# A second round trip through memory for the 256 inverse roots of a gated cross-attention kernel

## The chip, the cores and the metric

One core of one Trainium2 chip runs the kernel. The metric is the device time of one execution in microseconds (us); the time before is 291.95 us, the median of three runs (291.82 to 292.34). On a NeuronCore, TensorE (PE) multiplies matrices, VectorE (DVE) and ScalarE (ACT) work element by element, GpSimd (POOL) does a few small operations here, and SyncE (SP) issues every DMA of this kernel. Each engine runs its own list of instructions in order; engines wait for each other by semaphores.

## The reference

Everything is float32. `x` is 8 x 100 x 1024 (800 rows of width D = 1024), the context 8 x 722 x 512.

```
memory_proj = einsum('bme,de->bmd', memory, W_mem)
scores = einsum('bnd,bmd->bnm', x, memory_proj) / sqrt(D)
mc     = einsum('bnm,bmd->bnd', softmax(scores), memory_proj)
gate   = sigmoid(concat([x, mc]) @ W_gate.T + b_gate)
fused  = x + gate * mc
out    = fused * rsqrt(mean(fused**2, axis=-1) + 1e-6) * norm_w
```

Only the last two lines matter for the change: each of the 800 rows is divided by the root of its own mean square over 1024 columns.

## The kernel before

The kernel never forms `memory_proj`: it multiplies `x` with `W_mem` first, attends in the narrow width 512, and multiplies back. A float32 product is made of three matmuls of split operands (a high part and the rest, `act_hi`/`act_lo`, `w_turn_hi`/`w_turn_lo` and so on). The matrix work is ordered by hand, one list for each engine, with a semaphore for each hand-over.

The end of the program is the gate. The 800 rows fall into three sets:

- rows 0 to 415 (`FIRST`), the **first part**. Model columns lie on the 128 partitions in eight tiles, rows along the free axis;
- rows 416 to 671, the **second part**, 256 rows, in the same layout;
- rows 672 to 799, the **last rows**, 128 of them. Here rows lie on the partitions, and the model columns are worked in three groups of 384, 384 and 256 (`GROUPS`, steps NT, NT + 1 and LAST = NT + 2).

`STEPS` lists the sixteen gate steps of the first two sets, and three more follow for the last rows (`gate_rows`). At each step TensorE makes gate values in PSUM, ScalarE takes the sigmoid (`sigmoid`, lines 777 and 783), VectorE multiplies by `mc` and adds `x` (`gate_times` and `fuse`, lines 1019 and 1024; for the last rows `rows_times` and `rows_fuse`, lines 1046 and 1051), ScalarE squares (lines 814 and 807) and weighs with `norm_w`. For the last rows VectorE does the weighing (`rows_weigh`, line 1057).

For the two parts, the sum of squares runs over partitions, so a row's root has to be brought onto all 128 partitions before VectorE can multiply by it:

- First part: TensorE sums over partitions, VectorE adds the epsilon (line 1083), GpSimd raises to the power -0.5 (line 1151, `rooted`), SyncE stores the roots to a small buffer in device memory `rms_rows` (line 377), waits for that, and loads them back repeated on every partition into `rms_all` (line 379, signal `rms_in`). VectorE then multiplies the eight tiles (`output`, line 1030).
- Second part: two matmuls give the means (`means_second`, line 609), VectorE adds the epsilon (line 1102, `rms_late`), GpSimd takes the power (line 1153, `late_rooted`), and TensorE spreads the roots with two transposes of a broadcast column into a PSUM bank (`turn_roots`, line 616, `rms_turned`), after the first two of the eight blocks of three matmuls of step NT + 1. VectorE multiplies the eight tiles out of that bank (`output_second`, line 1035), five of them after the first group of the last rows, three after the second group.

After the last group VectorE adds up the mean of the last rows (`early_mean`, line 1118, and `rms_last`, line 1125), GpSimd takes the power (line 1155), and ScalarE and VectorE multiply a half each (lines 838 and 1134); two stores (line 390) end the program. The output of the second part leaves in four stores of two tiles each (line 385), each as soon as two products are done (`out_done`).

Of the kernel before, what the change touches and what calls it, by code (L numbers as in the profile page):

```python
# [7 lines left out]
P = 128  # L8
R = B * N
H = R // 2  # L10
KD, KC = D // P, C // P
# [12 lines left out]
FIRST, ROWS = 416, R - P  # L24

SLICES = ((FIRST, FIRST + P), (FIRST + P, ROWS))
# [16 lines left out]
NT = len(STEPS)  # L43
# [7 lines left out]
def build(nc, xT, x_last, ctxT, ctxN, w_mem, w_gate_x, w_mem_t, w_gate_mc, b_gate, norm_w, norm_row, outT, out_rows):  # L51
    F32, F32R = mybir.dt.float32, mybir.dt.float32r
    ALU, ACT, AX = mybir.AluOpType, mybir.ActivationFunctionType, mybir.AxisListType

    top = ExitStack()
    with top:  # L56
        def sb(scope, name, shape, dt=F32):
            return scope.enter_context(nc.sbuf_tensor(name, shape, dt))

        def sem(name):  # L60
            return top.enter_context(nc.semaphore(name))
# [12 lines left out]
        ident = sb(top, "ident", [P, P])  # L74
# [32 lines left out]
        rms_late = sb(top, "rms_late", [P, len(SLICES)])  # L107
# [3 lines left out]
        rms_all = sb(top, "rms_all", [P, TURNED])  # L111
        spread = sb(top, "spread", [P, P])
        same_lane = sb(top, "same_lane", [P, Q])
        square_part = sb(top, "square_part", [P, TURNED // Q])
        rms_rows = nc.dram_tensor("rms_rows", (FC, 4), F32, kind="Internal").ap()


# [22 lines left out]
        def bank(i, cols, rows=P, at=0):  # L140
            return ps[0:rows, i * BANK + at:i * BANK + at + cols]
# [7 lines left out]
        MEANS, RMS = 6, 7  # L149
# [8 lines left out]
        def group_cols(n):  # L158
            t0, t1 = GROUPS[n - NT]
            return slice(t0 * P, t1 * P)  # L160

        def in_tiles(cols):
            return cols.rearrange("p (t c) -> p t c", c=P)

        def gate_bank(n):
            if n >= NT:
                t0, t1 = GROUPS[n - NT]
                return bank(G2B + n % 2, (t1 - t0) * P)
            r0, r1 = STEPS[n][1:]
            return bank(G2B + n % 2, r1 - r0)  # L170
# [49 lines left out]
        squared, weighted = sem("squared"), sem("weighted")  # L220
# [6 lines left out]
        rooted, late_rooted = sem("rooted"), sem("late_rooted")  # L227
        rms_stored, rms_in = sem("rms_stored"), sem("rms_in")
        mean_w_set = sem("mean_w_set")
        late_mean_made = sem("late_mean_made")  # L230
        last_rooted, rms_turned = sem("last_rooted"), sem("rms_turned")
        out_done = sem("out_done")
# [12 lines left out]
        def _(sp):  # L245
# [134 lines left out]
            for k in range(0, KD, 2):  # L380
                sp.wait_ge(out_done, k + 2)
                sp.dma_start(out_v[:, k:k + 2, 0:FIRST], acc[:, k:k + 2, 0:FIRST]).then_inc(stored, 16)
            for k in range(0, KD, 2):
                sp.wait_ge(out_done, KD + k + 2)
                sp.dma_start(out_v[:, k:k + 2, FIRST:ROWS], acc[:, k:k + 2, FIRST:ROWS]).then_inc(stored, 16)
# [9 lines left out]
        def _(pe):  # L395
            def three(outs, weight, stream, first, last, onto=False):

                (wh, wl), done = weight, None
                for wgt, part in ((wh, 0), (wh, 1), (wl, 0)):
                    for h, o in enumerate(outs):  # L400
                        done = nc.tensor.matmul(o, wgt, stream[h][part],  # L401
                                                start=first and wgt is wh and part == 0,
                                                stop=last and wgt is wl, skip_group_check=onto)
                return done

            def w_tile(slot, i):
                return w_hi[slot][:, i * P:(i + 1) * P], w_lo[slot][:, i * P:(i + 1) * P]

            def halves(hi, lo, k):
                return [(hi[:, k, h * H:(h + 1) * H], lo[:, k, h * H:(h + 1) * H]) for h in range(2)]  # L410
# [8 lines left out]
            for k in range(KD):  # L419
# [24 lines left out]
                if k == 1:  # L444
# [5 lines left out]
                    for c in range(KC):  # L450
                        done = three([bank(c + 4, H)], w_tile(0, KC + c), halves(act_hi, act_lo, 1)[1:], False, False)
# [5 lines left out]
                if not last_k:  # L457
                    for c in range(KC):
                        done = three([bank(c, H), bank(c + 4, H)], w_tile(k // 2 % 2, k % 2 * 4 + c),
                                     halves(act_hi, act_lo, k), False, False)  # L460
                else:
                    for h in range(2):
                        for c in range(KC):
                            done = three([bank(c + 4 * h, H)], w_tile(k // 2 % 2, k % 2 * 4 + c),
                                         halves(act_hi, act_lo, k)[h:h + 1], False, True)
# [89 lines left out]
            for h in range(2):  # L555
                pe.wait_ge(at_lo_done, B // 2 if h == 0 else B)
                for k in range(KC):
                    done = three([bank(h, H)], w_tile(0, k), [halves(q_hi, q_lo, k)[h]], k == 0, k == KC - 1)
# [32 lines left out]
            def gate_rows(n, after=None, work=None):  # L591

                pe.wait_ge(seeded, n - 1)
                for k in range(KD):
                    xh, xl = act_hi[:, k, ROWS:R], act_lo[:, k, ROWS:R]
                    wh, wl = (a[:, :, k * P:(k + 1) * P] for a in w_groups[n - NT])
                    for act_part, w_part in ((xh, wh), (xh, wl), (xl, wh)):
                        done = nc.tensor.matmul(in_tiles(gate_bank(n)), act_part, w_part,  # L598
                                                start=False, stop=k == KD - 1 and act_part is xl,
                                                skip_group_check=True)  # L600
                    if k == after:
                        work()
                done.then_inc(gate_made, 1)
# [5 lines left out]
                    done = nc.tensor.matmul(late_mean(i), square_sum[:, a:b], mean_w[:, :], start=True, stop=True)  # L609
                done.then_inc(late_mean_made, 1)  # L610

            def turn_roots():

                pe.wait_ge(late_rooted, 1)
                for i in range(len(SLICES)):
                    done = nc.tensor.transpose(bank(RMS, P, P, i * P), rms_late[:, i:i + 1].to_broadcast([P, P]),
                                               ident[:, :])
                done.then_inc(rms_turned, 1)

            for n in range(END0 + 2):  # L620
                gate_mc(n)
            gate_mc(END0 + 2, 6, mean_first)
            for n in range(END0 + 3, NT):
                gate_mc(n)
            gate_rows(NT, 6, means_second)
            gate_rows(NT + 1, 1, turn_roots)
            gate_rows(NT + 2)


# [213 lines left out]
        def _(dve):  # L843
            def minus(out, whole, hi):
                return nc.vector.tensor_tensor(out, whole, hi.bitcast(F32), ALU.subtract)  # L845
# [64 lines left out]
            for h in range(2):  # L910
                for c in range(KC):
                    dve.wait_ge(q_hi_done, h * KC + c + 1)
                    done = minus(q_lo[:, c, h * H:(h + 1) * H], bank(c + 4 * h, H),
                                 q_hi[:, c, h * H:(h + 1) * H]).then_inc(q_lo_done, 1)
# [117 lines left out]
            def output_second(k):  # L1032

                rows = acc[:, k, FIRST:ROWS]
                nc.vector.tensor_tensor(rows, rows, bank(RMS, ROWS - FIRST), ALU.mult).then_inc(out_done, 1)

            def turn_mc():

# [4 lines left out]
            def rows_times(n):  # L1043
                part = in_tiles(gate[:, n % 2, 0:group_cols(n).stop - group_cols(n).start])
                dve.wait_ge(gate_done, n + 1)
                nc.vector.tensor_tensor(part, part, last_rows(mc, n - NT), ALU.mult).then_inc(gated, 1)

            def rows_fuse(n):
                cols = group_cols(n)
                dve.wait_ge(gated, n + 1)  # L1050
                nc.vector.tensor_tensor(fused_rows[:, cols], gate[:, n % 2, 0:cols.stop - cols.start],
                                        fused_rows[:, cols], ALU.add).then_inc(fused, 1)

            def rows_weigh(n):
                cols = group_cols(n)
                dve.wait_ge(fused, n + 1)
                nc.vector.tensor_tensor(row_out[:, cols], fused_rows[:, cols], norm_rows[:, cols],
                                        ALU.mult).then_inc(rows_weighted, 1)
# [22 lines left out]
            for g in range(4):  # L1081
                lanes = slice(g * Q, (g + 1) * Q)
                done = nc.vector.tensor_scalar(rms[lanes, :], bank(MEANS, TURNED // Q)[lanes, 4 * g:4 * g + 4], EPS, None,
                                               ALU.add)
            done.then_inc(mean_copied, 1)
            fuse(END0 + 1)
            done = 0
# [17 lines left out]
            dve.wait_ge(rows_in, 32)  # L1105
            rows_times(NT)
            rows_fuse(NT)
            dve.wait_ge(weighted, NT)
            dve.wait_ge(rms_turned, 1)
            for k in range(5):  # L1110
                output_second(k)
            rows_times(NT + 1)
            rows_fuse(NT + 1)
            for k in range(5, KD):
                output_second(k)
            rows_weigh(NT)
            dve.wait_ge(squared, NT + 2)
            nc.vector.tensor_scalar(early_mean[:, :], last_mean[:, 0:1], last_mean[:, 1:2], EPS, ALU.add, ALU.add)\
                .then_inc(early_mean_set, 1)
# [69 lines left out]
```

## Time and profile before

| what | value |
|---|---|
| median of three runs | 291.95 us (291.82 to 292.34) |
| the profiled execution, its own time | 292.03 us |
| its span in the trace | 290.2 us |
| PE, PEld busy | 283.0 us (97%), 272.5 us (94%) |
| DVE, ACT, POOL busy | 180.3 us (62%), 160.1 us (55%), 4.7 us (2%) |
| DMA | 55.46 MB, mean 191 GB/s |

The trace covers 290.2 us of the 292.03 us; the 1.8 us around it are not in the trace. A busy share is an average over stages that differ: whether an engine matters at the end of the program must be read from the end. The chain of waits, followed back from the last instruction, says which work ended last; the timeline by engine shows starts, durations and, in brackets, how long the engine had been idle and who released it.

### The profile page before, as it was taken

What the parts mean: (1) busy time and instruction counts of PE and PEld (TensorE: products, weight loads), DVE (VectorE), ACT (ScalarE), POOL (GpSimd) and SP (SyncE); (2) the same over time, 40 slices, a digit from 0 to 9 for tenths busy, and PEclk for the clock granted to TensorE, in tenths of its full rate; (3) what the DMA queues carried; (4) which work ended last, traced back from release to release, by engine and by line L of the source; (5) the groups of instructions that cost most, each with busy time, mean ns of one, the idle gap of its engine ahead of it and who ended that gap; (6) DMA issues with size and microseconds to landing.
All of it is one profiled execution on the core that took longest, in us unless ns stands there. A gap on an engine that the chain in (4) does not pass through costs nothing.

```text
span 290.2 us, 4178 instructions
## 1 busy us (share of the span) xinstructions
PE 283.0 (97%) x1643; PEld 272.5 (94%) x1643; DVE 180.3 (62%) x261; ACT 160.1 (55%) x233; POOL 4.7 (2%) x11
## 2 busy tenths in 40 slices
PE   8999999999999999999999999999999999999991
PEld 8999999898998989899898999999999999999990
DVE  3757663668667586775759563364347765476764
ACT  4648353556493745739465545534546864656632
POOL 2000000000000000000000000000000000010000
PEclk9999999999999999999999999999999999999996
DMA  6999290696988889797796720239706511622334
GB/s 205 389 404 283 93 354 2 169 291 207 320 215 224 248 241 318 183 341 225 213 299 216 158 70 11 72 104 373 190 12 225 189 23 66 130 89 95 117 134 145
DMA packets 51331, 55.46 MB, mean 191 GB/s; under 512 B 29760, under 2 KB 34624, under 8 KB 51312
## 3 DMA queue, kind: packets, MB, share of 16 engines
q1 hardware_dynamic: 51312, 55.19, 61.2%
q8 instruction: 13, 0.21, 0.3%
q14 instruction: 6, 0.05, 0.1%
HBM read 48.76 MB, written 6.16 MB: 189 GB/s over the span
## 4 chain that ended last, share of the span: by engine, by line
PE 95%; issue 3%; POOLq 0%; POOL 0%; ACT 0%; ACTq 0%; DVE 0%
PE ps L401 67%; PE ps L496 11%; PE ps L521 10%; PE ps L510 1%; PE ps L525 1%; PE ps L598 1%; PE ps L415 1%; PE ps L427 0%; PE ps L430 0%; PE ps L433 0%; PE ps L437 0%; PE ps L439 0%; PE ps L442 0%; POOLq L56 0%; POOL rms_late L1153 0%
## 5 line engine op out<-in xcount | busy, mean ns | idle before, releaser
L401 PE MATMUL ps<-act_hi,w_turn_hi 128*128 128x400 f32 (+2 forms) x216 | 60.4, 342 | 0.0
L401 PE MATMUL ps<-act_lo,w_turn_hi 128*128 128x400 f32 (+2 forms) x216 | 59.8, 340 | 0.0
L401 PE MATMUL ps<-act_hi,w_turn_lo 128*128 128x400 f32 (+2 forms) x216 | 59.7, 339 | 0.0
L401 PEld LDWEIGHTS ps<-act_hi,w_turn_hi 128*128 128x128 f32 x216 | 39.4, 188 | 0.9
L401 PEld LDWEIGHTS ps<-act_lo,w_turn_hi 128*128 128x128 f32 x216 | 40.0, 188 | 0.1
L401 PEld LDWEIGHTS ps<-act_hi,w_turn_lo 128*128 128x128 f32 x216 | 40.0, 188 | 0.0
L845 DVE TENSOR_TENSOR w_turn_lo<-w_stage,w_turn_hi 128x1024 fp32r<-128x1024 f32 (+2 forms) x20 | 22.3, 1116 | 23.3 <-ACT w_turn_hi L639 23.0
L845 DVE TENSOR_TENSOR cn_lo<-cn_stage,cn_hi 128x1536 fp32r<-128x1536 f32 (+1 forms) x16 | 23.8, 1486 | 5.6 <-ACT cn_hi L658 5.0
L845 DVE TENSOR_TENSOR ct_lo<-ct_stage,ct_hi 128x1444 fp32r<-128x1444 f32 x16 | 25.8, 1653 | 0.5 <-ACT ct_hi L650 0.5
L708 ACT ACTIVATE probs<-ps,neg_top 100x722 f32<-100x722 f32 x8 | 6.9, 866 | 27.2 <-DVE neg_top L926 27.2
L639 ACT ACTIVATE w_turn_hi<-w_stage 128x1024 fp32r<-128x1024 f32 x17 | 17.9, 1053 | 6.9 <-PE ps L401 5.1
L650 ACT ACTIVATE ct_hi<-ct_stage 128x1444 fp32r<-128x1444 f32 x16 | 21.7, 1410 | 0.0
L496 PE MATMUL ps<-ct_hi,q_lo 128*100 128x362 f32 x64 | 21.0, 328 | 0.0
L496 PE MATMUL ps<-ct_hi,q_hi 128*100 128x362 f32 x64 | 20.9, 327 | 0.0
L496 PE MATMUL ps<-ct_lo,q_hi 128*100 128x362 f32 x64 | 20.9, 327 | 0.0
L730 ACT ACTIVATE pc<-ps,row_inv 100x512 f32<-100x512 f32 x8 | 5.5, 688 | 25.3 <-PE ps L525 25.3
L845 DVE TENSOR_TENSOR act_lo<-mc,act_hi 128x800 fp32r<-128x800 f32 x8 | 7.9, 991 | 18.1 <-ACT mc L756 18.1
L401 PE MATMUL ps<-q_hi,w_turn_hi 128*128 128x400 f32 x64 | 17.5, 344 | 0.0
L401 PE MATMUL ps<-q_lo,w_turn_hi 128*128 128x400 f32 x64 | 17.5, 343 | 0.0
L401 PE MATMUL ps<-q_hi,w_turn_lo 128*128 128x400 f32 x64 | 17.4, 343 | 0.0
L783 ACT ACTIVATE gate_square<-ps,bias_t 128x256 f32<-128x256 f32 (+1 forms) x14 | 7.4, 529 | 17.2 <-PE ps L401 17.2
L1019 DVE TENSOR_TENSOR gate_square<-gate_square,mc 128x416 f32<-128x416 f32 (+1 forms) x16 | 8.1, 506 | 13.8 <-ACT gate_square L783 13.8
(151 smaller groups left out, 572.3 us busy)
## 6 DMA issues: line engine op xcount, KB each, us to landing
ct_stage<-ctxT SPq DMA_DIRECT2D x16, 722.0 KB, 8.2
cn_stage<-ctxN SPq DMA_DIRECT2D x8, 768.0 KB, 7.3
cn_stage<-ctxN SPq DMA_DIRECT2D x8, 512.0 KB, 4.3
w_stage<-w_gate_x SPq DMA_DIRECT2D x8, 512.0 KB, 6.2
w_stage<-w_gate_mc SPq DMA_DIRECT2D x8, 512.0 KB, 3.5
x_again<-xT SPq DMA_DIRECT2D x1, 2688.0 KB, 11.1
cn_stage<-ctxN SPq DMA_DIRECT2D x8, 320.0 KB
acc<-xT SPq DMA_DIRECT2D x6, 400.0 KB, 7.4
```

Source lines behind the costliest of these rows:

```text
L401: done = nc.tensor.matmul(o, wgt, stream[h][part], start=first and wgt is wh and part == 0, stop=last and wgt is wl, skip_group_check=onto)
L415: nc.tensor.matmul(bank(7, P), ones, ones, start=True, stop=True)
L496: done = nc.tensor.matmul(bank(h, MH + 1, N), lhs[:, k, b * N:(b + 1) * N], rhs[:, k, at:at + MH + 1], start=k == 0 and part == 0, stop=k ...
L510: done = nc.tensor.transpose(o, probs[:, t * P:t * P + rows], ident[0:N, 0:N])
L521: nc.tensor.matmul(bank(PCB, C, N), lhs[:, t, :], rhs[:, t, :], start=t == 0 and part == 0, stop=False)
L639: nc.scalar.activation(hi[:, :], w_stage[:, slot, :], ACT.Copy).then_inc(w_hi_done, 1)
L650: nc.scalar.activation(ct_hi[:, 2 * s:2 * s + 2, :], ct_stage[:, 2 * s:2 * s + 2, :], ACT.Copy).then_inc(ct_hi_done, 1)
L708: nc.scalar.activation(probs[:, :].rearrange("p (h m) -> p h m", h=2), scores, ACT.Exp, bias=neg_top[:, :], scale=float(D) ** -0.5, accum_ ...
L730: nc.scalar.activation(pc[0:N, :], bank(PCB, C, N), ACT.Copy, scale=row_inv[:, :]).then_inc(pc_scaled, 1)
L783: nc.scalar.activation(part, part if n < 2 else gate_bank(n), ACT.Sigmoid, bias=bias_t[:, t:t + 1]).then_inc(gate_done, 1)
L845: return nc.vector.tensor_tensor(out, whole, hi.bitcast(F32), ALU.subtract)
L1019: nc.vector.tensor_tensor(part, part, mc[:, t, r0:r1], ALU.mult).then_inc(gated, 1)
```

## The change

The two transposes on TensorE go. In their place SyncE stores the second part's 256 roots from `rms_late` (128 partitions by 2) to a new buffer in device memory, `rms_second`, and loads them back repeated onto all partitions into the first 256 columns of `rms_all`. Both transfers are issued after the first part's stores and ahead of the second part's. The load waits for the store, and for `out_done` to reach eight, since the first part's products read `rms_all`. VectorE's products of the second part read `rms_all` in place of PSUM and are issued as one row of eight, after the second group of the last rows; `rows_weigh(NT)` moves ahead of that group.

```diff
+        rms_second = nc.dram_tensor("rms_second", (len(SLICES), P), F32, kind="Internal").ap()
...
             for k in range(0, KD, 2):
                 sp.wait_ge(out_done, k + 2)
                 sp.dma_start(out_v[:, k:k + 2, 0:FIRST], acc[:, k:k + 2, 0:FIRST]).then_inc(stored, 16)
+            sp.wait_ge(late_rooted, 1)
+            sp.dma_start(rms_second.rearrange("i p -> p i"), rms_late[:, :], allow_slow_non_contiguous=True)\
+                .then_inc(rms_stored, 16)
+            sp.wait_ge(rms_stored, 32)
+            sp.wait_ge(out_done, KD)
+            sp.dma_start(rms_all[:, 0:ROWS - FIRST], rms_second.rearrange("i p -> (i p)").partition_broadcast(P))\
+                .then_inc(rms_in, 16)
             for k in range(0, KD, 2):
                 sp.wait_ge(out_done, KD + k + 2)
                 sp.dma_start(out_v[:, k:k + 2, FIRST:ROWS], acc[:, k:k + 2, FIRST:ROWS]).then_inc(stored, 16)
...
-            def turn_roots():
-
-                pe.wait_ge(late_rooted, 1)
-                for i in range(len(SLICES)):
-                    done = nc.tensor.transpose(bank(RMS, P, P, i * P), rms_late[:, i:i + 1].to_broadcast([P, P]),
-                                               ident[:, :])
-                done.then_inc(rms_turned, 1)
-
...
-            gate_rows(NT + 1, 1, turn_roots)
+            gate_rows(NT + 1)
...
                 rows = acc[:, k, FIRST:ROWS]
-                nc.vector.tensor_tensor(rows, rows, bank(RMS, ROWS - FIRST), ALU.mult).then_inc(out_done, 1)
+                nc.vector.tensor_tensor(rows, rows, rms_all[:, 0:ROWS - FIRST], ALU.mult).then_inc(out_done, 1)
...
             rows_times(NT)
             rows_fuse(NT)
-            dve.wait_ge(weighted, NT)
-            dve.wait_ge(rms_turned, 1)
-            for k in range(5):
-                output_second(k)
+            rows_weigh(NT)
             rows_times(NT + 1)
             rows_fuse(NT + 1)
-            for k in range(5, KD):
+            dve.wait_ge(weighted, NT)
+            dve.wait_ge(rms_in, 32)
+            for k in range(KD):
                 output_second(k)
-            rows_weigh(NT)
             dve.wait_ge(squared, NT + 2)
```

VectorE's list near its end, from the product of the first group of the last rows (L1046) on, the difference between before (-) and the change (+). `gate_square` holds the gate values, `w_stage` the fused last rows, `x_again` their weighed form; `ps` is PSUM.

```order
 L1046 TENSOR_TENSOR gate_square<-gate_square,mc 128x384 [waits gate_done,rows_in,mc_rows_in]
 L1051 TENSOR_TENSOR w_stage<-gate_square,w_stage 128x384 [waits gated]
-L1035 TENSOR_TENSOR acc<-acc,ps 128x256 [waits rms_turned,weighted]
-L1035 TENSOR_TENSOR acc<-acc,ps 128x256 x4
+L1057 TENSOR_TENSOR x_again<-w_stage 128x384 [waits fused]
 L1046 TENSOR_TENSOR gate_square<-gate_square,mc 128x384 [waits gate_done]
 L1051 TENSOR_TENSOR w_stage<-gate_square,w_stage 128x384 [waits gated]
-L1035 TENSOR_TENSOR acc<-acc,ps 128x256 x3
-L1057 TENSOR_TENSOR x_again<-w_stage 128x384 [waits fused]
-L1118 TENSOR_SCALAR early_mean<-last_mean 128x1 [waits squared]
+L1035 TENSOR_TENSOR acc<-acc,rms_all 128x256 [waits rms_in,weighted]
+L1035 TENSOR_TENSOR acc<-acc,rms_all 128x256 x7
```

All eight products now stand between the second group (second L1046, L1051) and `early_mean`; five of them stood a group earlier. The wait for the roots moves with them, and the weighing L1057 of the first group moves ahead.

SyncE's list from the first load of roots on, before:

```order
L379 DMA rms_all<-rms_rows 128x512 [waits rms_stored]
L382 DMA outT<-acc 128x2x416 [waits out_done] x4
L385 DMA outT<-acc 128x2x256 [waits out_done] x4
L390 DMA out_rows<-x_again 128x512 [waits row_right,row_left] x2
L56 UNCONDITIONAL_BRANCH [waits stored]
```

and in the change:

```order
L380 DMA rms_all<-rms_rows 128x512 [waits rms_stored]
L383 DMA outT<-acc 128x2x416 [waits out_done] x4
L385 DMA rms_second<-rms_late 128x2x1 [waits late_rooted]
L389 DMA rms_all<-rms_second 128x256 [waits out_done,rms_stored]
L393 DMA outT<-acc 128x2x256 [waits out_done] x4
L398 DMA out_rows<-x_again 128x512 [waits row_right,row_left] x2
L56 UNCONDITIONAL_BRANCH [waits stored]
```

Two transfers come in between the two sets of output stores, and nothing else moves on this queue.

## Rows read from the trace of the kernel before

**Rows 1.** The page: busy time by engine, and the time in 40 slices.

```profile
PE 283.0 (97%) x1643; PEld 272.5 (94%) x1643; DVE 180.3 (62%) x261; ACT 160.1 (55%) x233; POOL 4.7 (2%) x11
...
PE   8999999999999999999999999999999999999991
```

**Rows 2.** The chain that ended last, from 270 us: start, length (us), what.

```profile
271.84 3.67 PE ps L598 x21
...
276.12 0.71 POOL rms_late L1153
276.82 9.02 issue
285.85 0.71 POOLq L56
```

**Rows 3.** Timeline of TensorE: start, duration, operation, tiles, [idle before, releaser].

```profile
277.02 0.33 PE L598 MATMUL ps<-q_lo,act_hi 128*128 128x384 f32 x1
277.19 0.34 PE L598 MATMUL ps<-q_hi,act_lo 128*128 128x384 f32 x1
277.37 0.38 PE L616 MATMUL ps<-ident,rms_late 128*128 128x128 f32 x2
277.50 0.42 PE L598 MATMUL ps<-q_hi,act_hi 128*128 128x384 f32 x1
277.76 0.34 PE L598 MATMUL ps<-q_lo,act_hi 128*128 128x384 f32 x1
...
283.46 0.28 PE L598 MATMUL ps<-w_turn_hi,act_lo 128*128 128x256 f32 x1
```

**Rows 4.** Timeline of ScalarE, the last rows' sigmoids and squares.

```profile
280.93 0.49 ACT L777 ACTIVATE gate_square<-ps 128x384 f32<-128x384 f32 x1 [1.99 <-PE ps L598]
...
283.77 0.38 ACT L777 ACTIVATE gate_square<-ps 128x256 f32<-128x256 f32 x1 [0.51 <-PE ps L598]
```

**Rows 5.** Timeline of VectorE, the end of the program.

```profile
277.73 0.56 DVE L1051 TENSOR_TENSOR w_stage<-gate_square,w_stage 128x384 f32<-128x384 f32 x1
278.21 1.74 DVE L1035 TENSOR_TENSOR acc<-acc,ps 128x256 f32<-128x256 f32 x5
281.45 0.56 DVE L1046 TENSOR_TENSOR gate_square<-gate_square,mc 128x384 f32<-128x384 f32 x1 [1.51 <-ACT gate_square L777]
282.05 0.56 DVE L1051 TENSOR_TENSOR w_stage<-gate_square,w_stage 128x384 f32<-128x384 f32 x1
282.52 1.07 DVE L1035 TENSOR_TENSOR acc<-acc,ps 128x256 f32<-128x256 f32 x3
283.52 0.55 DVE L1057 TENSOR_TENSOR x_again<-w_stage 128x384 f32<-128x384 f32 x1
283.99 0.20 DVE L1118 TENSOR_SCALAR early_mean<-last_mean 128x1 f32<-128x1 f32 x1
284.19 0.43 DVE L1046 TENSOR_TENSOR gate_square<-gate_square,mc 128x256 f32<-128x256 f32 x1
...
285.64 0.16 DVE L1125 TENSOR_TENSOR rms_last<-last_mean,early_mean 128x1 f32<-128x1 f32 x1
```

**Rows 6.** Timeline of VectorE, operations of 256 columns with all operands in SBUF.

```profile
264.29 0.42 DVE L1024 TENSOR_TENSOR acc<-gate_square,x_again 128x256 f32<-128x256 f32 x1
264.63 0.42 DVE L1007 TENSOR_TENSOR square_sum<-square_sum,gate_square 128x256 f32<-128x256 f32 x1
265.05 1.09 DVE L1030 TENSOR_TENSOR acc<-acc,rms_all 128x416 f32<-128x416 f32 x2
```

**Rows 7.** Timeline of GpSimd, the first and the second part's powers.

```profile
257.99 1.19 POOL L1151 TENSOR_TENSOR rms<-rms,minus_half 128x4 f32<-128x4 f32 x1 [255.06 <-DVE rms L1083]
276.12 0.71 POOL L1153 TENSOR_TENSOR rms_late<-rms_late,minus_half 128x2 f32<-128x2 f32 x1 [16.94 <-DVE rms_late L1102]
```

**Rows 8.** Timeline of SyncE: when a DMA is issued.

```profile
259.21 0.33 SPq L377 DMA_DIRECT2D rms_rows<-rms  x1
261.80 0.32 SPq L379 DMA_DIRECT2D rms_all<-rms_rows  x1
275.55 0.37 SPq L382 DMA_DIRECT2D outT<-acc  x1
...
287.12 0.82 SPq L390 DMA_DIRECT2D out_rows<-x_again  x2
```

**Rows 9.** DMA issues: count, KB each, us from issue to landing.

```profile
outT<-acc SPq DMA_DIRECT2D x1, 416.0 KB, 3.4
...
outT<-acc SPq DMA_DIRECT2D x4, 256.0 KB, 2.2
...
rms_all<-rms_rows SPq DMA_DIRECT2D x1, 256.0 KB, 3.2
...
rms_rows<-rms SPq DMA_DIRECT2D x1, 2.0 KB, 2.6
```

**Rows 10.** DMA in 262 to 265 us, in 40 slices of 0.075 us.

```profile
DMA  0000000000051445776775745446442311000000
```

**Rows 11.** DMA in 275.9 to 280 us, in 40 slices of 0.1 us.

```profile
GB/s 0 0 0 0 0 211 357 390 341 406 373 406 373 390 406 260 65 16 32 16 32 16 32 16 16 0 0 0 0 0 0 0 0 0 0 0 0 0 60 290
```

**Rows 12.** The DMAs of `pc_mem`, a store and reload inside the busy attention stage.

```profile
DMA to landing us min/median/max: 1.9/5.6/6.8
```

## The prediction

> **What bounds the kernel now.** I read the page first: TensorE is busy for 97% of the span, and in the 40 slices it is full up to the last one [rows 1]. So nothing that VectorE or a DMA does matters before about 284 us unless TensorE waits for it, and the question moves to the last slice. Next the chain of waits: it runs through TensorE's matmuls and then shows 9.02 us of "issue" from 276.82 to the last power on GpSimd [rows 2]. That stretch is where the inference of releasers gives up, so I follow it by the engines' timelines instead. TensorE issues its last matmul at 283.46; it ends near 283.74 [rows 3]. ScalarE's last sigmoid starts at 283.77, released by it, and ends at 284.15 [rows 4]. VectorE starts the product of the last group at 284.19 [rows 5]. From there a fixed chain leads to the end: sum, square, mean, power, the halves, two stores, the first of them issued at 287.12 [rows 8].
>
> The reader is to see one thing in rows 5: VectorE is not idle ahead of 284.19. The three products from 282.52, the weighing of a group from 283.52 and `early_mean` from 283.99 follow each other without a gap, and `early_mean` ends at 284.19. The sigmoid is ready at 284.15. So two paths meet at 284.19 with about 0.04 us between them: TensorE's, and VectorE's. VectorE has no slack there, and what the change puts on it ahead of that point goes into the time one for one.
>
> **What leaves TensorE.** The matmuls of the last rows start 0.17 us apart (277.02 to 277.19). Across the two transposes the step from 277.19 to 277.76 is 0.57 us, where two ordinary steps take 0.35 us [rows 3]. The transposes cost 0.22 us. Without them the second group's sigmoid comes at 280.71 in place of 280.93 [rows 4], VectorE's product and sum of that group run at 281.23 and 281.83, and VectorE is free at 282.30 in place of 282.52 [rows 5]. The last group's sigmoid would end at 283.93.
>
> **What moves on VectorE.** Five products used to run from 278.21 to 279.95 in a gap: VectorE then idled 1.51 us until the second group's sigmoid [rows 5]. That cover was free. Now all eight products stand between 282.30 and the last group. The weighing of the first group (0.47 us from its start to the next operation's, 283.52 to 283.99) moves into the gap in their place; it starts near 278.2 and ends long before 281.2, so it costs nothing there.
>
> A product out of PSUM has a pitch of 0.33 us: five take 1.74, of which the last is a full 0.41, so (1.74 - 0.41) / 4; with three it is (1.07 - 0.41) / 2 [rows 5]. The new products read SBUF alone. The nearest row is an operation of the same size with SBUF operands only: 264.29 to 264.63, 0.34 us [rows 6]. Two SBUF products of 416 columns take 1.09 us, the second starting about 0.51 us after the first, no faster by size. I take 0.335 us for each, 2.68 us for eight. `early_mean` adds 0.20 us [rows 5].
>
> If the roots were there at once: 282.30 + 2.68 + 0.20 = 285.18, against 284.19. That is **+0.99 us**, with TensorE's gain of 0.22 us already in it. The last sigmoid, at 283.93, now waits 1.2 us for VectorE. The gain on TensorE becomes idle time of the chain.
>
> The Trainium skill's page "VectorE: DVE Perf Modes", in its section on the TRN2 errata, gives a fixed cost of 58 cycles to a VectorE operation from SBUF and 120 from PSUM at 0.96 GHz. By it a product out of SBUF would be 65 ns cheaper and eight of them 0.52 us; the sum would be +0.47 us. The two pitches above (0.33 out of PSUM, 0.34 out of SBUF) speak against it.
>
> **The round trip.** SyncE is free when the roots are made: the first part's last store is issued at 275.55 and takes 0.37 us to issue [rows 8]. The power ends at 276.12 + 0.71 = 276.83 [rows 7]. In the first part SyncE issued its store 0.03 us after the power (257.99 + 1.19 = 259.18, then 259.21), so the new store is issued at 276.86. The first part's store landed after 2.6 us and its load was issued 2.59 us after the store [rows 8, 9]. The new store differs in two ways. It has 256 pieces of 4 bytes in place of 128 of 16, and it stands behind a store of 416 KB that took 3.4 us and whose bytes trickle at 16 to 32 GB/s from 277.6 to 278.4, where 340 to 406 GB/s had flowed [rows 9, 11]. Lower bound 2.6 us. Upper bound 3.5 us, by adding those 0.9 us of trickle; a far bound is the 5.6 us median of the small stores and loads of `pc_mem`, made in the middle of heavy loading that is absent here [rows 12]. I take 3.0 us, near the row of the same pattern.
>
> The load repeats 1 KB on 128 partitions; the first part's repeats 2 KB and lands after 3.2 us [rows 9]. Its bytes move from 262.8 to 264.6, about 1.75 us [rows 10]; half of them leave 3.2 - 0.9 = 2.3 us. Bounds are 2.2 us (a 256 KB store, rows 9) and 3.2 us. I take 2.6 us. The roots land at 276.86 + 3.0 + 2.6 = 282.5; bounds 281.7 and 283.6. VectorE is free at 282.30, so the round trip is nearly hidden and adds 0.2 us, with bounds of 0 and 1.3 us.
>
> The page "DMA: Bandwidth & Descriptors" of the Trainium skill gives a DMA about 2.0 us fixed plus bytes at 436 GB/s. By it the trip takes 4.3 us, the roots land at 281.2 and the sum stays at +0.99. The first part's own trip, 2.59 + 3.2 us, is longer.
>
> **What else is issued.** SyncE waits in the new trip with nothing behind it but the second part's stores, which cannot go before their products. They are now issued near 283.3, 283.9, 284.6 and 285.3; each lands after 2.2 us [rows 9], the last near 287.5. The last rows' stores go out at 287.12 + 1.2 = 288.3, past them. Nothing for that.
>
> **The sum.** Against 284.19: -0.22 (transposes), +1.68 (eight products in the path, 2.68, in place of three, 1.00), -0.47 (the weighing moved into the gap), +0.20 (the roots late, from 282.30 to 282.5). That is **+1.2 us**, 285.4 for the start of the last group's product. The profiled execution took 292.03 us, 0.08 above the median of 291.95. So 293.2 us.
>
> **Rivals.**
> - *The round trip decides.* The 4-byte pieces or the store ahead cost more, and the roots land between 282.9 and 284.4. For it: no row shows such a store. Against it: the first part's row and the quiet queue. Each microsecond after 282.3 counts in full: +1.6 to +3.1 us, 293.6 to 295.1 us. VectorE would show an idle time ahead of its first product, released by the DMA.
> - *Products out of SBUF are cheaper*, so eight take 2.15 us and a prompt trip gives +0.5 us, 292.5 us, within what can be told from no change. For it: the pitch of these very products is not in the trace. Against it: the same size and operation out of SBUF keeps 0.34 us [rows 6]. It is the case that the page's fixed costs describe.
> - *TensorE alone sets the end, and the change is faster.* Mechanism: the last group's product starts when its sigmoid is ready, 0.22 us earlier, 291.8 us. It holds if eight products and `early_mean` fit between 282.30 and 283.97, that is if a product takes under 0.18 us. The rows say 0.335. The change does what it says, but the gain has nowhere to go.
>
> **How the numbers follow.** About 0.2% (0.58 us) is what a measurement of this kernel can tell from no change. Forecast (start of the products 282.3 to 282.9, +1.0 to +1.6 us): 0.73. Round trip decides: 0.20. Cheaper products: 0.05. TensorE's end: 0.02. So faster 0.02, same 0.05, slower 0.93. The range goes from 292.8, the forecast's lower end less some noise, to 294.5, which takes in most of the late-trip case.
>
> **What would show it.** In the profile after: no L616 rows and the last sigmoid near 283.55; the roots' load issued near 279.9 and landed near 282.5; eight products in a row from 282.3 to 282.9 with a pitch of 0.33 to 0.34 us; `early_mean` near 285.2; the last group's product near 285.4 with the sigmoid long done; a span near 291.4 us. The prediction is wrong if VectorE is free ahead of the last sigmoid, if it waits for the DMA by over 0.6 us, or if the pitch out of SBUF is not that of rows 6.

## The result, and the profile after

The changed kernel takes 301.12 us (median of four runs, 301.05 to 302.36) against 291.98 us for the kernel before on the same chip. The ratio is 1.0323, 95% interval 1.0308 to 1.0338: 9.1 us more where I had forecast 1.2 and had left nothing above 294.5 us. The direction was right, the size was wrong by more than a factor of seven.

The profiled execution took 301.05 us, with a span of 299.2 us. The page after shows TensorE with about the same work, over a longer span:

```profile
PE 282.3 (94%) x1641; PEld 271.9 (91%) x1641; DVE 180.2 (60%) x261; ACT 160.2 (54%) x233; POOL 4.7 (2%) x11
...
PE   8999999999999999999999999999999999999800
```

Two slices at the end are now empty of TensorE [rows 1 for before]. The waits from 262 us on (engine and line, what it waited for: us in total, times, longest) name the place at once, for VectorE and, in the second pair of rows, for SyncE's queue:

```profile
DVE acc L1035 <- DMA rms_all<-rms_second: 8.5, 1, 8.5
...
DVE x_again L1132 <- POOL rms_last L1153: 0.4, 1, 0.4
...
SPq L389 <- DMA rms_second<-rms_late: 10.0, 1, 10.0
...
SPq L56 <- DMA out_rows<-x_again: 1.9, 1, 1.9
```

VectorE's timeline at the end, the counterpart of [rows 5]:

```profile
277.87 0.56 DVE L1057 TENSOR_TENSOR x_again<-w_stage 128x384 f32<-128x384 f32 x1
280.77 0.56 DVE L1046 TENSOR_TENSOR gate_square<-gate_square,mc 128x384 f32<-128x384 f32 x1 [2.34 <-ACT gate_square L777]
281.37 0.56 DVE L1051 TENSOR_TENSOR w_stage<-gate_square,w_stage 128x384 f32<-128x384 f32 x1
290.38 2.77 DVE L1035 TENSOR_TENSOR acc<-acc,rms_all 128x256 f32<-128x256 f32 x8 [8.46 <-DMA rms_all<-rms_second]
293.07 0.20 DVE L1116 TENSOR_SCALAR early_mean<-last_mean 128x1 f32<-128x1 f32 x1
293.20 0.41 DVE L1046 TENSOR_TENSOR gate_square<-gate_square,mc 128x256 f32<-128x256 f32 x1
```

VectorE idles 8.46 us ahead of its first product, and the wait ends with the load. ScalarE's last sigmoid was done long before:

```profile
283.09 0.38 ACT L777 ACTIVATE gate_square<-ps 128x256 f32<-128x256 f32 x1 [0.51 <-PE ps L606]
```

SyncE's timeline and the DMA issues (count, KB, us from issue to landing), the counterparts of [rows 8, 9], split the trip:

```profile
276.40 0.49 SPq L385 DMA_DIRECT2D rms_second<-rms_late  x1
286.97 0.34 SPq L389 DMA_DIRECT2D rms_all<-rms_second  x1
```

```profile
rms_all<-rms_second SPq DMA_DIRECT2D x1, 128.0 KB, 3.3
...
rms_rows<-rms SPq DMA_DIRECT2D x1, 2.0 KB, 3.2
rms_second<-rms_late SPq DMA_DIRECT2D x1, 1.0 KB, 10.6
```

A store of 1 KB takes 10.6 us. The DMA activity shows what it does in that time. These are two windows, 275.9 to 280 us (the rate in slices of 0.1 us, then the packets) and 280 to 284 us (the packets):

```profile
GB/s 65 260 422 308 455 373 390 357 406 390 373 179 33 16 34 22 35 16 32 0 0 0 0 0 0 0 0 0 0 0 0 0 0 0 0 0 0 0 0 0
DMA packets 544, 0.43 MB, mean 104 GB/s; under 512 B 288, under 2 KB 544, under 8 KB 544
...
DMA packets 1, 0.01 MB, mean 2 GB/s; under 512 B 0, under 2 KB 0, under 8 KB 0
```

The small packets have all passed by 278.0 us (nearly all of the 256 pieces by 277.7, the last sixteen packets at 277.9). Then the queue carries nothing, and the store's landing is signalled at 286.97. It is not waiting for its turn or moving bytes: nine of its 10.6 microseconds lie between the last packet and the signal that the writes have landed.

The 416 KB store ahead of it, issued at 275.10, is held up with it. It landed after 11.7 us, at 286.8, where the same store landed after 3.4 us before [rows 9]:

```profile
outT<-acc SPq DMA_DIRECT2D x1, 416.0 KB, 11.7
```

Nothing waited for that store here, so it cost nothing.

The account against the 284.19 of before: by the chain of waits, the stretch of the last rows' matmuls began 0.46 us earlier in this execution (271.38 against 271.84). The store took 7.6 us more than I took for it, the load 0.7 us more; the products and `early_mean` took what was forecast within 0.1 us. 1.2 - 0.46 + 7.6 + 0.7 = 9.0, and 293.20 - 284.19 = 9.01.

### The profile page after: what moved, and what is told of

Same layout as the page of the kernel before. It is cut to its first block, busy times and chain, and to the rows that moved or that the text cites. A ratio compares the mean times of both kernels' runs of the same rounds, so it can differ in the third digit from the quotient of the medians.

```text
span 299.2 us, 4177 instructions
## 1 busy us (share of the span) xinstructions
PE 282.3 (94%) x1641; PEld 271.9 (91%) x1641; DVE 180.2 (60%) x261; ACT 160.2 (54%) x233; POOL 4.7 (2%) x11
## 4 chain that ended last, share of the span: by engine, by line
PE 92%; issue 6%; POOLq 0%; POOL 0%; ACT 0%; ACTq 0%; DVE 0%
PE ps L409 65%; PE ps L504 11%; PE ps L529 9%; PE ps L518 1%; PE ps L533 1%; PE ps L606 1%; PE ps L423 1%; PE ps L435 0%; PE ps L441 0%; PE ps L445 0%; PE ps L450 0%; PE ps L438 0%; PE ps L447 0%; POOLq L56 0%; POOL rms_late L1151 0%
## 5 line engine op out<-in xcount | busy, mean ns | idle before, releaser
L754 ACT ACTIVATE act_hi<-ps 128x800 fp32r<-128x800 f32 x8 | 6.7, 840 | 17.7 <-PE ps L409 17.7
```

Of the source, the lines that this page charges most:

```text
L754: nc.scalar.activation(act_hi[:, bass.ds(k, 1), :].rearrange("p k (h r) -> p (k h) r", h=2), src, ACT.Copy)
```

## The experiments

The question is why a store of 256 pieces of 4 bytes takes 10.6 us where one of 128 pieces of 16 bytes takes 2.6. Theory A: it is the spacing in memory; pieces that fall close together are taken one after the other. Theory C: a 4-byte piece is dear wherever it goes. Theory D: it is the 416 KB store ahead in the queue. Beside it stands the rest of my sum, which needs its own test. The edits are shown shortened, and against the changed kernel unless the text says otherwise. The time of the kernel before that stands beside a version is the median of its executions on the same chip; 64, 16 and 8 bytes apart, half the pieces, pairs, the quiet queue and the change once more are one execution each. Five of these (64, 16 and 8 bytes apart, half the pieces, pairs) load the first part's roots in place of the new ones: they give wrong values for the second part and are read for their times only. That load, from a buffer written long before, also took 2.8 to 2.9 us, where loads of the freshly stored 1 KB took 3.3 to 4.6. So their totals can be a few tenths better than those of a real trip.

**8 bytes a lane.**

```diff
-rms_second: (len(SLICES), P)
+rms_second: (P, len(SLICES))
-sp.dma_start(rms_second.rearrange("i p -> p i"), rms_late[:, :], ...)
+sp.dma_start(rms_second, rms_late[:, :])
-nc.vector.tensor_tensor(rows, rows, rms_all[:, 0:ROWS - FIRST], ALU.mult)
+roots = rms_all[:, 0:ROWS - FIRST].rearrange("p (q i) -> p i q", q=P)
+nc.vector.tensor_tensor(rows, rows, roots, ALU.mult)
```

> The changed kernel, with the roots kept as (lane, slice) in memory: the store writes 128 pieces of 8 bytes in place of 256 of 4, and VectorE reads the loaded roots with a step of two. Theory A (writes into the same small stretch of memory are taken one after the other, some 37 ns each, (286.96 - 277.5) / 256): half the writes, so the store lands after about 5.5 to 6 us in place of 10.6, the roots are there near 286, 296 to 297 us. Theory C (only a piece of 4 bytes is dear, as less than some unit): the store lands after 2.6 to 3.2 us like the first part's 16-byte pieces, 293 to 294 us, my forecast for the change. Theory D (the queue, the store standing behind 416 KB): no change, 301 us. If VectorE pays for the step of two, its pitch rises from 0.336 us.

Measured 294.78 us, ratio 1.0079 (1.0064 to 1.0094), +2.3 us. The store landed after 3.8 us:

```profile
rms_all<-rms_second SPq DMA_DIRECT2D x1, 128.0 KB, 3.3
...
rms_second<-rms_late SPq DMA_DIRECT2D x1, 1.0 KB, 3.8
```

The layout alone is worth 6.8 us of 10.6 (4.4 against the shortest crowded store below, 8.2). D falls: the queue ahead is the same. My fixed 37 ns for each write falls too, since by it half the writes would have left 5.5 to 6 us. With roots read at a step of two the pitch stayed at (286.83 - 284.14) / 8 = 0.336 us:

```profile
284.14 2.77 DVE L1036 TENSOR_TENSOR acc<-acc,rms_all 128x256 f32<-128x256 f32 x8 [1.66 <-DMA rms_all<-rms_second]
286.83 0.20 DVE L1117 TENSOR_SCALAR early_mean<-last_mean 128x1 f32<-128x1 f32 x1
```

**Each piece 64 bytes from the next.**

```diff
-rms_second: (len(SLICES), P)
+rms_second: (len(SLICES), P, 16), written at [:, :, 0]
-load from rms_second
+load from the first 256 values of rms_rows
```

> The changed kernel with each of the 256 pieces of 4 bytes written 64 bytes from the next (16 KB in all). The load repeats the first part's roots, so that the second part's outputs use wrong roots: only the time is read. Theory A (same stretch of memory): the store lands after 2.6 to 4 us. Theory C (4-byte pieces are dear wherever they go): 10 us or so again. Theory D (the queue ahead): 10 us again.

292.67 us against 292.35 for before. The store landed after 2.4 us, with the same 256 pieces of 4 bytes. C falls.

```profile
282.05 2.76 DVE L1035 TENSOR_TENSOR acc<-acc,rms_all 128x256 f32<-128x256 f32 x8
...
rms_second<-rms_late SPq DMA_DIRECT2D x1, 1.0 KB, 2.4
```

VectorE no longer waits for the roots at all. The last group's product starts at 284.86, 4.40 us after the second group's sigmoid (280.46), where before it was 3.26 (284.19 - 280.93, rows 4 and 5): +1.14 on VectorE, -0.22 on TensorE, +0.92 together.

**Half the pieces, as close as in the change.**

```diff
-rms_second: (len(SLICES), P)
+rms_second: (P, 1)
-store rms_late[:, :]
+store rms_late[:, 0:1]
-load from rms_second
+load from the first 256 values of rms_rows
```

> The changed kernel, storing only one of the two columns of roots: 128 pieces of 4 bytes next to each other (512 bytes). The second half of the roots is not stored, and the load repeats the first part's roots, so the values of the second part are not the reference's. Theory A with a cost for each write: 5.5 to 6 us to landing. If the number of pieces does not matter and only their size does (C): 10 us. D: 10 us.

298.7 us against 292.35 for before; the store took 8.4 us:

```profile
rms_second<-rms_late SPq DMA_DIRECT2D x1, 0.5 KB, 8.4
```

Half as many pieces in half as many bytes save little or nothing (256 pieces took 8.2 to 10.6 us, as the runs below show); a cost for each write would have halved it.

**4 bytes, 16 bytes apart; and 8 bytes apart.** As the 64-byte case, with the last dimension 4 and 2 in place of 16.

> The changed kernel, 256 pieces of 4 bytes each 16 bytes from the next (4 KB in all); the load repeats the first part's roots, so the second part's roots are wrong ones. Theory A, in the form that x1, x2 and x3 leave (what counts is how many pieces fall within 64 bytes: 16 gave 10.6 and 8.4 us, 8 gave 3.8, 1 gave 2.4): four pieces in 64 bytes, as in the first part's store (2.6 to 3.2 us), so 2.6 to 3.5 us. Rival C' (the size of the piece against its neighbour: 4-byte pieces are dear unless each has a line of its own): 5 us or more.

> As x5, with 8 bytes from one piece to the next (2 KB in all): eight pieces in 64 bytes, as in x1, but of 4 bytes and twice as many. Theory A by pieces in 64 bytes: 3.8 to 5 us to landing. C' (the size of the piece): near 8 to 10 us.

16 bytes apart the store took 2.6 us (293.45 us in all against 292.13), 8 bytes apart 3.8 us (294.08 us). The rows of the two:

```profile
rms_second<-rms_late SPq DMA_DIRECT2D x1, 1.0 KB, 2.6
```

```profile
rms_second<-rms_late SPq DMA_DIRECT2D x1, 1.0 KB, 3.8
```

At eight bytes from start to start, 256 pieces of 4 bytes took the same 3.8 us as 128 pieces of 8 bytes. Neither size nor number of pieces explains the times, and the distance between their starts does.

**Pairs.**

```diff
+for i in range(len(SLICES)):
+    sp.dma_start(rms_second[:, i:i + 1], rms_late[:, i:i + 1], ...)   # rms_second: (P, 4)
-load from rms_second
+load from the first 256 values of rms_rows
```

> The changed kernel with the 256 pieces of 4 bytes in pairs: two stores of 128 pieces at a pitch of 16 bytes, the second's beside the first's, so that 8 pieces lie in 64 bytes as in x8, but two of them in each 8 bytes. The load repeats the first part's roots, so the second part's roots are wrong ones. If only the number of pieces in 64 bytes counts: about 3.8 us from the first store's issue, plus 0.4 us for the second's issue, so 4.2 us. If it is two pieces in one 8 bytes that is dear: 8 us or more.

294.42 us against 291.85 for before. From the first store's issue at 276.87 to the load's at 280.85 it took 3.98 us:

```profile
276.87 0.82 SPq L386 DMA_DIRECT2D rms_second<-rms_late  x2
280.85 0.32 SPq L390 DMA_DIRECT2D rms_all<-rms_rows  x1
```

Two neighbours 4 bytes apart are not dear by themselves, as long as 64 bytes hold eight pieces in place of sixteen. That fits a cost that goes by how many pieces crowd into a stretch. It is not shown beyond doubt, since the two stores were issued some 0.4 us apart and the neighbours did not go out together. How long the stretch is these runs don't tell: eight to 64 bytes is also four to 32.

**The store held back until the queue is quiet.**

```diff
 sp.wait_ge(late_rooted, 1)
+sp.wait_ge(stored, 64)
```

> The changed kernel, the store of the roots held until the first part's four stores have landed (some 2 us later). Theory A: its own time stays near 10 us, the roots come 2 us later and the whole takes 302 to 303.5 us. Theory D (the 416 KB ahead of it make it slow): 3 us to landing, and about 295.5 us.

302.21 us against 292.13. The store was issued at 278.67, with the 416 KB landed and its queue empty, and landed after 8.2 us, the load after 4.6 us:

```profile
rms_all<-rms_second SPq DMA_DIRECT2D x1, 128.0 KB, 4.6
...
rms_second<-rms_late SPq DMA_DIRECT2D x1, 1.0 KB, 8.2
```

Quiet takes nothing like 7 us away. Whether it takes 2.4 us needed the next run.

**The change once more.** No edit.

> The changed kernel once more, for the spread of its store: 10.6 us in its profile, 8.2 us when it was held until the queue was quiet. If the store ahead of it costs those 2.4 us, again 10 to 11 us; if a dense store simply varies, anything from 8 to 11.

299.46 us against 291.85 for before; the store 8.6 us, with the 416 KB ahead of it as before:

```profile
rms_all<-rms_second SPq DMA_DIRECT2D x1, 128.0 KB, 3.5
...
rms_second<-rms_late SPq DMA_DIRECT2D x1, 1.0 KB, 8.6
```

The crowded store varies from 8.2 to 10.6 us over four executions, one of them with 128 pieces. So 8.2 in the quiet queue shows no gain from the quiet. What makes it vary was not tested. The 416 KB store ahead landed late here too, after 9.8 us (9.6 with half the pieces, 4.7 to 4.9 in the two versions with starts 8 bytes apart, 3.1 to 3.7 in all others): whatever holds up the crowded store, the store ahead waits with it.

**VectorE's order alone, transposes kept** (on the kernel before).

```diff
-output_second for k in 0..4, rows_times/rows_fuse(NT + 1), output_second for k in 5..7, rows_weigh(NT)
+rows_weigh(NT), rows_times/rows_fuse(NT + 1), output_second for k in 0..7
```

> The kernel before with its transposes on TensorE, and only VectorE's order of the change: the weighing of the first group ahead, all eight products after the second group, out of PSUM. By the prediction's sum without TensorE's gain and without the round trip: 1.68 - 0.47 = +1.2 us, 293.1 to 293.3 us. If VectorE has slack that I did not see, under +0.5 us. If the order is what cost 9 us, about 301 us.

293.20 us against 292.35, ratio 1.0029 (1.0018 to 1.0041): +0.85 us, interval +0.5 to +1.2, against 1.2 forecast. The trace holds the steps:

```profile
282.48 2.73 DVE L1035 TENSOR_TENSOR acc<-acc,ps 128x256 f32<-128x256 f32 x8
285.13 0.21 DVE L1116 TENSOR_SCALAR early_mean<-last_mean 128x1 f32<-128x1 f32 x1
285.26 0.41 DVE L1046 TENSOR_TENSOR gate_square<-gate_square,mc 128x256 f32<-128x256 f32 x1
```

285.26 stands where 284.19 stood, +1.07. So the new order by itself costs some 1 us, with no round trip in it. The pitch out of PSUM is (2.73 - 0.41) / 7 = 0.33 us, that of the change out of SBUF (2.77 - 0.42) / 7 = 0.336 us [rows 5, 6].

**All eight products in the gap.**

```diff
-for k in range(5): output_second(k)
+for k in range(KD): output_second(k)
+rows_weigh(NT)
 rows_times(NT + 1)
 rows_fuse(NT + 1)
-for k in range(5, KD): output_second(k)
-rows_weigh(NT)
```

(on the kernel before)

> The kernel before with all eight products and the weighing of the first group placed in VectorE's gap between the first two groups (2.68 + 0.47 = 3.15 us from 278.2, against a gap to 281.45). If TensorE's path sets the end, as I read it, at most 0.04 us is won: 291.8 to 292.0 us. If VectorE was the later path by more than that, up to 0.5 us is won. If the products run past 281.45 and delay the second group's sum, a few tenths are lost only if VectorE comes after the last sigmoid, which it should not.

292.18 us against 292.13, ratio 1.0002 (0.9993 to 1.0011): no difference.

```profile
281.47 0.56 DVE L1046 TENSOR_TENSOR gate_square<-gate_square,mc 128x384 f32<-128x384 f32 x1
...
283.31 0.21 DVE L1116 TENSOR_SCALAR early_mean<-last_mean 128x1 f32<-128x1 f32 x1 [0.69 <-ACT gate_square L807]
284.21 0.42 DVE L1046 TENSOR_TENSOR gate_square<-gate_square,mc 128x256 f32<-128x256 f32 x1 [0.68 <-ACT gate_square L777]
```

VectorE now has 0.68 us of idle time ahead of the last group's product, and that product starts at 284.21, as before. The time is TensorE's there. In the kernel before the two paths met within 0.1 us, and TensorE's came last: where nothing holds the last group's product up, it follows `early_mean` by 0.13 us (285.13 to 285.26 in the run above), so VectorE would have been free at 283.99 + 0.13 = 284.12, ahead of the sigmoid's end at 284.15.

**The first part's shape of trip.**

```diff
-rms_late: [P, 2], rms_second: (len(SLICES), P)
+rms_late: [P, 4] (two columns idle), rms_second: (P, 4)
+sp.dma_start(rms_second, rms_late[:, :])
+sp.dma_start(rms_all[:, :], rms_second.rearrange("p i -> (p i)").partition_broadcast(P))
+roots = rms_all[:, :].rearrange("p (q i) -> p i q", q=P)[:, 0:2, :]
```

> The change with the first part's own shape of round trip: rms_late is widened to four columns (two of them idle), so that the store writes 128 pieces of 16 bytes and the load repeats 2 KB; VectorE reads the roots with a step of four. Theory A (spacing in memory): the store lands after 2.6 to 3.2 us, the load after 3.2, the roots are there near 283, and the whole is 1.6 to 2.0 us above the kernel before, the case that the prediction priced. If something else in the new trip is slow, more than 3 us above it.

294.92 us, ratio 1.0106 (1.0089 to 1.0123), +3.1 us: more than expected, and not for the trip. The store landed after 2.3 us, the load after 3.4, the roots were there at 282.4. The eight products took 4.28 us:

```profile
282.45 4.28 DVE L1037 TENSOR_TENSOR acc<-acc,rms_all 128x256 f32<-128x256 f32 x8 [0.25 <-DMA rms_all<-rms_second]
286.65 0.20 DVE L1118 TENSOR_SCALAR early_mean<-last_mean 128x1 f32<-128x1 f32 x1
```

That is a pitch of (286.65 - 282.45) / 8 = 0.525 us in place of 0.336, 1.5 us more for the eight.

**The roots packed once** (added to the version above).

```diff
+nc.vector.tensor_copy(square_sum[:, 0:256] as (i q), rms_all[:, :] as (q i), i in 0..1)
-nc.vector.tensor_tensor(rows, rows, roots, ALU.mult)
+nc.vector.tensor_tensor(rows, rows, square_sum[:, 0:ROWS - FIRST], ALU.mult)
```

> x10_first_pattern with one VectorE copy that packs the 256 roots side by side before the eight products. If the step of four in the roots is what raised the pitch from 0.336 to 0.53 us in x10, it falls back to 0.336, at the price of one copy of 0.3 to 0.5 us: 1.0 to 1.3 us less than x10, 293.4 to 294.0 us, the trip and the products as the prediction priced them. If the pitch came from the queue of output stores or from TensorE beside it, it stays at 0.53 us and the whole is 0.3 to 0.5 us above x10.

293.59 us, ratio 1.0056 (1.0035 to 1.0076), +1.6 us.

```profile
282.53 0.39 DVE L1114 COPY square_sum<-rms_all 128x256 f32<-128x256 f32 x1
282.96 2.77 DVE L1036 TENSOR_TENSOR acc<-acc,square_sum 128x256 f32<-128x256 f32 x8
285.65 0.21 DVE L1120 TENSOR_SCALAR early_mean<-last_mean 128x1 f32<-128x1 f32 x1
```

The pitch is back at 0.336 us: the step of four in the operand had raised it. Less the 0.43 us that the copy takes, this is the change with a trip of ordinary length, some +1.2 us.

The stores side by side:

| distance of starts | pieces | issue to landing, us |
|---|---|---|
| 4 bytes | 256 of 4 bytes (three executions) | 10.6, 8.6, 8.2 |
| 4 bytes | 128 of 4 bytes | 8.4 |
| 8 bytes | 128 of 8 bytes | 3.8 |
| 8 bytes | 256 of 4 bytes | 3.8 |
| 16 bytes | 256 of 4 bytes | 2.6 |
| 16 bytes | 128 of 16 bytes, the new trip (two versions) | 2.3, 2.1 |
| 16 bytes | 128 of 16 bytes, the first part's own store, all versions | 2.5 to 3.2 |
| 64 bytes | 256 of 4 bytes | 2.4 |

No version here beats the kernel before. The best with a round trip and the right roots is +1.6 us. With the roots there in time the new order still loses about 1 us by the traces (+0.3 us in the total of the one execution 64 bytes apart, +0.85 us for the order alone).

## Why the prediction was wrong, step by step

- **What bounds the end.** Right but for 0.07 us. VectorE's and TensorE's paths meet near 284.19; moving all products into the gap changed nothing, and work added to VectorE counted from 284.12 on. The prediction took the 0.20 us from `early_mean` to the next product as the operation's own cost. It is 0.13 us, and the rest was the wait for the sigmoid.
- **The transposes, -0.22 us.** Right. From the start of the last rows' matmuls, as the chain has it, to the last sigmoid it took 283.77 - 271.84 = 11.93 us before and 283.09 - 271.38 = 11.71 us after. The gain became idle time, as forecast.
- **The products, 0.335 us each, no cheaper out of SBUF.** Right, 0.336. The rule of the Trainium skill's page "VectorE: DVE Perf Modes" on fixed costs (its section on the TRN2 errata), by which PSUM would be 65 ns dearer for each product, does not show in back-to-back products of this size: 0.33 against 0.336 us.
- **Eight products in the path, +0.99 us with the roots at once.** Right within 0.1 by the traces: +1.14 - 0.22 = +0.92 in the 64-byte run. In the packed run the last group's product starts 4.86 us after the second sigmoid (285.77 - 280.91), against 3.26 before: less the copy's 0.43 and TensorE's 0.22, +0.95. The 0.07 us above is the difference.
- **The store, "I take 3.0 us, near the row of the same pattern", upper bound 3.5.** This is the step that failed: 10.6 us. The prediction named both differences, 4-byte pieces and the store ahead, and priced only the second. It called the row that of the same pattern. What mattered is where the pieces land: the first part's lie 16 bytes apart, the new ones 4. The far bound of 5.6 us was not even far enough, and it was kept out of the range for being in another stage. No row of before shown there held writes this close, so the honest upper end was open. Why the close writes land late stays open.
- **The load, 2.6 us, by halving the time of the bytes.** Wrong by 0.7 us. The load of half the bytes took 3.3. In the runs that load 1 KB from `rms_rows` it took 2.8 to 2.9, where 2 KB took 3.0 to 3.2 in the same executions, so halving the bytes saves 0.1 to 0.4 us and not 0.9. The other 0.4 us or more came only with roots stored just before, 3.3 to 4.6 us in four executions; why is not shown. The page "DMA: Bandwidth & Descriptors" of the Trainium skill, by whose figures the prediction had the whole trip at 4.3 us, fits them on DMAs issued by GpSimd; here SyncE issues, and the two trips with 16-byte pieces took 5.7 and 5.4 us.
- **The rival "the round trip decides".** The right mechanism, with its sign in the trace (VectorE idle, released by the DMA), at three times the upper end of the price it was given.

There was a hint in the trace before that the prediction did not use. The rate in 258 to 262 us, in slices of 0.1 us, shows the first part's small store, issued at 259.21:

```profile
GB/s 0 0 0 0 0 0 0 0 0 0 0 0 0 0 0 0 0 164 0 0 9 10 1 0 0 0 1 1 0 0 0 0 0 0 0 0 0 0 0 0
```

The 164 in one slice is a fetch of instructions. Most of the store's bytes pass at 260.0 to 260.3 and a few at 260.6 to 260.8, yet it lands at 261.8. So a microsecond of its 2.6 lay behind the last byte already. I took the 2.6 us as the price of a small store, where a part of it belonged to how the writes end.

## What to carry to other kernels

Before a small tensor goes to memory and back, look at the distance between the starts of its pieces in memory: here, within one store, 4 bytes cost 8.2 to 10.6 us, 8 bytes 3.8, 16 bytes and more 2.1 to 3.2, for the sizes (4 to 16 bytes) and numbers (128 and 256) tried. A crowded store also delays the landing of the store ahead of it, which matters where something waits for that one. Price an engine's queue by its order as well: moving five short products out of a gap into the stretch before the last wait cost 1 us, five times what the freed TensorE time could give. And when an unseen operation differs from its nearest row in a way that no row prices, leave the upper end open rather than take the bound from the difference that can be priced.

## What the hardware showed that I had not expected

- The crowded store sends its packets within some 0.6 us (277.4 to 278.0) and lands nine microseconds later, while the queue carries nothing; the 416 KB store ahead of it, in flight beside it, lands only then too. The page "DMA: Bandwidth & Descriptors" of the Trainium skill says in its specifications that below 512 bytes the DMA engine does a read-modify-write. If so, writes to one small stretch could have to wait for each other, and the run of times by distance agrees in direction; no run shows it. Small pieces alone are not it: those of 4 bytes at 16 and 64 bytes' distance landed after 2.6 and 2.4 us. What the memory really does there, and over what length, these runs do not show. Nor do they show whether it matters that pieces come from different DMA engines.
- A float32 operand read at a step of four raised VectorE's product of 256 columns from 0.336 to 0.525 us; at a step of two it stayed at 0.336. The page "SBUF — State Buffer" of the Trainium skill speaks in its specifications of 16-byte lines that want two hits each; a float32 operand has two in a line at a step of two and one at a step of four. Both runs agree with it.
- A load that repeats one row on 128 partitions hardly gets cheaper with half the bytes: 2.8 to 2.9 us for 1 KB, 3.0 to 3.2 for 2 KB. The number of reads was 128 in both, so its share is not shown. Loads of 1 KB stored just before took longer, 3.3 to 4.6 us.
